# Four chained transformer layers on one core: attention scores by 64x64 quarters, two tiles at once, in layers 1 and 3; layer 2's loop written out; the end of layer 0 re-ordered

## The chip, the cores and the metric

The kernel runs on one core of a Trainium2 chip. The time is that of the device, in microseconds (us), and smaller is better. Three runs of the kernel before took 2104.95 to 2109.8 us, with a median of 2108.38 us.

## The reference

Sixty-four sequences of 64 tokens with 256 features pass through four layers, all in float32. Each layer normalises its rows, scales and shifts them by vectors made from a conditioning input, runs attention over the 64 tokens of each sequence, adds the result, and then does the same with an MLP of 1024 hidden features. What differs:

```python
# layer 0: one head of 256; RMS norm; GELU
scores = jnp.einsum('bnd,bmd->bnm', Q, K) * D ** (-0.5)
# layer 1: 16 heads of 16; RMS norm; rotary embedding of q and k; SwiGLU
q = _rope(q.reshape(B, T, n_head, hd)).transpose(0, 2, 1, 3)
k = _rope(k.reshape(B, T, n_head, hd)).transpose(0, 2, 1, 3)
attn = jnp.einsum('bhqd,bhkd->bhqk', q, k) * (1.0 / np.sqrt(hd))
# layer 2: 16 heads of 64 (qkv of 3 x 1024); layer norm; gated residual
attn = jnp.einsum('bqhd,bkhd->bhqk', q, k) * scale
# layer 3: 16 heads of 16; layer norm; padding mask; gated residual
mask = padding_mask[:, None, :] & padding_mask[:, :, None]
attn = jnp.where(mask[:, None, :, :], attn, -1000000000.0)
```

## The kernel before, in words

All rows (`xres`) stay in SBUF. They are cut into 8 blocks of 512 rows: 8 sequences, or 4 tiles of 128 rows. Eight phases follow each other, attention and MLP of the four layers (`PHASES`, line 52; phase 4 is layer 2's attention), and each phase goes over its 8 blocks. Weights of the next phase are loaded in shares and split by GpSimd into a rounded part and a rest (`share`, `split_next`, line 1307), and each projection is three matmuls, of rest by rounded, rounded by rest and rounded by rounded (`project`, line 630).

The order of the work is written by hand: `order_of` (line 78) returns for each kind of phase a list of stages. Each stage is marked as belonging to this block (`own`), the one before (`prev`) or the one after (`nxt`). `run_phases` (line 376) walks that list once per block, and every engine walks the same list and issues what its part of a stage is. So the list fixes the order on each engine, and semaphores (`n_at` gives the values) do the rest. The first and the last block of a phase are written out and the six between them are a loop (`Fori`, line 413); phase 0 is written out whole (line 406). At a phase's end the remaining `prev` stages are run inside the next phase, and `UP_AFTER` (line 145) says behind which of them the next MLP's first two `up` products go.

Attention of layers 1 and 3 has 8 steps a block, called slots here: slot k begins at `own("scores", k)`. Half c = k // 4 of the features (128 of 256, 8 heads) goes with tile j = k % 4 (two sequences). In a slot:

- PE makes the scores of tile k into its own PSUM bank, `scores[k % 2]`. The stationary operand is `qb`, q of one sequence with the heads of odd or even number zeroed (two copies, side by side). The moving operand is `kx`, which holds k of the sequence four times, each copy with only one group of 32 features (two heads) left and zeros elsewhere. So one product of 128 by 128 with 256 columns gives all eight heads, for one sequence (lines 727 to 730). In layer 3 a product of mask rows is added first (line 725).
- VectorE takes the maximum over keys (line 1217) and writes the scores less the maximum to `pb` (line 1220), then frees the bank.
- PE turns `pb` of the tile before (`probs_t`, line 741), ScalarE takes exp while it copies it to `pt` (line 994), PE multiplies with the values (`pv`, line 760; each head has a 17th column of ones), and VectorE divides after every second tile (lines 1239 and 1244).

Once a block: statistics (`stats`, line 1131; GpSimd makes rstd, line 1352), `norm` (line 1149 in layer 1, 1151 in layer 3), `turn` (PE transposes, line 675; VectorE scales, line 1159; GpSimd adds, line 1357), `split` (ScalarE `h_hi`, line 897; VectorE `h_lo`, line 1170), the projections q, k and v, `merge` of the heads (lines 782, 1001, 1251), `proj`, and `back` (PE line 826, VectorE line 1297, adds to `xres`). In layer 1 q and k are also rotated: ScalarE writes rows (line 903), SyncE swaps neighbouring partitions by DMA (line 545), VectorE multiplies by the cosine (line 1178), GpSimd by the sine and adds (lines 1362 and 1368). ScalarE's `q_out` makes the two copies of `qb` (line 965); `k_out` makes `kx` in four operations of 32 partitions (lines 950 and 959). Before the first use `kx` is zeroed by ScalarE (`zero_part`, line 852).

Layer 2 (heads of 64) already makes its scores with 64x64 quarters of the PE array (lines 712 to 719): 16 products a step, which the trace counts as 32 instructions, and its values likewise (line 774). In layer 0's last block GpSimd divides (line 1376), splits weights (`share`) and adds a bias to `xres` (`bias`, line 1386).

Of the kernel before, what the change touches and what calls it, by code (L numbers as in the profile page):

```python
# [77 lines left out]
def order_of(kind, layer):  # L78
# [37 lines left out]
    if layer == 3:  # L116
        return [own("mask", 1), own("scores", 0), prev("probs_t", 7), own("q", 1), own("q_out", 1), prev("pv", 6), own("share"), nxt("load"),
                own("scores", 1), own("probs_t", 0), own("v", 0), prev("pv", 7), own("v_out", 0), own("v", 1),
                own("v_out", 1), nxt("stats"),
                own("scores", 2), nxt("norm"), own("probs_t", 1), prev("merge"), own("k", 1), own("k_out", 1), own("pv", 0),  # L120
                own("scores", 3), own("probs_t", 2), prev("proj"), own("pv", 1), nxt("turn"),
                own("scores", 4), own("probs_t", 3), prev("back"), nxt("split"), own("pv", 2),
                own("scores", 5), nxt("mask", 0), own("probs_t", 4), own("pv", 3), nxt("k", 0), nxt("k_out", 0),
                own("scores", 6), own("probs_t", 5), own("pv", 4), nxt("q", 0), nxt("q_out", 0),
                own("scores", 7), own("pv", 5), own("probs_t", 6)]
# [17 lines left out]
TABLE_BANKS = (3, 5)  # L143

UP_AFTER = {0: [("probs_t", 0), ("pv", 0)], 1: [("merge", 0), ("proj", 0)],
# [19 lines left out]
def counts_of(kind, layer):  # L165
# [16 lines left out]
    if layer in (1, 3):  # L182
        c.update(o_full=n, o_inv=n // 2, o_free=n // 2, q=2 * 2, k=4 * 2, v=2 * 2, q32=2, w_full=3, w_free=1, att_hi=2, att=2)
    if layer == 1:
        c.update({f"{s}_{what}": 64 if what == "swapped" else 2 for s in "qk" for what in ("rows", "cos", "swapped", "sin")})
        c.update(k32=2)
# [11 lines left out]
def build(nc, x_in, cond_in, mask_k_in, mask_q_in, vec_in, modw_in, weights_in, out, phases=len(PHASES)):  # L198
# [13 lines left out]
    with ExitStack() as ctx:  # L212
# [18 lines left out]
        zeroed = ctx.enter_context(nc.semaphore("zeroed"))  # L231
        mask_made = ctx.enter_context(nc.semaphore("mask_made"))
# [40 lines left out]
        no_seq = place("no_seq", [P, 2], F32)  # L273
        mx = place("mx", [P, 2, SEQ], F32)
# [559 lines left out]
        def _(act):  # L834
# [36 lines left out]
            def stage_of(ph, s, k, b):  # L871
# [4 lines left out]
                if kind == "mlp" and layer in (0, 2) and s == "up" and k >= 3 and is_first(b):  # L876
                    if k == 3:
                        act.wait_ge(sem["x_done"], n_at("x_done", ph, 0, 1))
# [611 lines left out]
```

## Time and profile before

| | value |
|---|---|
| median of three runs | 2108.38 us |
| the profiled execution | 2108.39 us, span 2106.6 us |
| PE busy | 1998.5 us (95%), 15460 matmuls |
| VectorE, ScalarE, GpSimd busy | 1301.5, 1018.7, 439.5 us |
| layer 0 attention, MLP | about 137 and 208 us |
| layer 1 attention, MLP | about 288 and 267 us |
| layer 2 attention, MLP | about 534 and 206 us |
| layer 3 attention, MLP | about 269 and 198 us |
| mean granted clock of PE | 0.988 |

PE is the matmul side of TensorE, PEld its weight loads, DVE is VectorE, ACT ScalarE, POOL GpSimd, SP SyncE. Busy time of PE overlaps from one matmul to the next, so the distance between two starts says more than a duration. The clock is the share of 2.4 GHz that was granted; 0.5 is 1.2 GHz.

### The profile page before, as it was taken

The numbers are of one execution on the slowest core, as the hardware profiler recorded it, in microseconds if no ns is written. First come the engines' busy times: TensorE is split into PE (matmuls) and PEld (weight loads), VectorE is DVE, ScalarE is ACT, GpSimd is POOL, SyncE is SP. The second block draws the span as 40 slices with busy tenths as digits, with TensorE's granted clock in tenths as the row PEclk, the third lists the DMA queues.
The fourth block names the chain that finished last, engine by engine and source line by source line (L and its number), as shares of the span: only waits on it lengthen the run. The fifth ranks groups of instructions, "written<-read, shape, count | busy, mean of one in ns | idle before, by whom it ended". The sixth has DMA issues, their size and how long they took to land.

```text
span 2106.6 us, 44526 instructions
## 1 busy us (share of the span) xinstructions
PE 1998.5 (95%) x15460; PEld 1639.1 (78%) x15460; DVE 1301.5 (62%) x2506; ACT 1018.7 (48%) x1623; POOL 439.5 (21%) x409
## 2 busy tenths in 40 slices
PE   8989998989899999999999989998999999999998
PEld 7977887777777888877777777776888778787887
DVE  6665665777775656545544555555666777775664
ACT  4436555565643333335444444445446645554453
POOL 4441113445430101011111111111011321210000
PEclk9989999999999999999999999999999999999999
DMA  6000000111110000000000000000000000000000
GB/s 230 16 15 8 7 11 28 46 37 45 37 38 11 20 10 20 10 11 7 2 5 7 6 7 1 5 4 13 6 7 8 11 6 10 10 0 11 20 20 30
DMA packets 23959, 42.06 MB, mean 20 GB/s; under 512 B 2354, under 2 KB 13106, under 8 KB 23474
## 3 DMA queue, kind: packets, MB, share of 16 engines
q1 hardware_dynamic: 23858, 40.65, 5.8%
q8 instruction: 71, 1.16, 0.2%
q14 instruction: 30, 0.25, 0.0%
HBM read 28.06 MB, written 4.19 MB: 15 GB/s over the span
## 4 chain that ended last, share of the span: by engine, by line
PE 80%; DVE 8%; issue 7%; ACT 3%; POOL 1%; DVEq 0%; DMA 0%; ACTq 0%; POOLq 0%; SPq 0%
PE psum L633 21%; PE psum L635 19%; PE psum L634 19%; PE psum L728 4%; PE psum L741 3%; PE psum L675 3%; PE psum L760 2%; PE psum L826 2%; DVE xn L1149 2%; PE psum L774 2%; PE psum L717 1%; DVE pb L1220 1%; DVE mx L1217 1%; PE psum L564 1%; DVE h_lo L1170 1%
## 5 line engine op out<-in xcount | busy, mean ns | idle before, releaser
L633 PE MATMUL psum<-h_hi,w_lo 128*128 128x512 f32 x1056 | 433.9, 411 | 18.3 <-DVE h_lo L1170 7.6
L635 PE MATMUL psum<-h_hi,w_hi 128*128 128x512 f32 x1056 | 414.6, 393 | 0.0
L634 PE MATMUL psum<-h_lo,w_hi 128*128 128x512 f32 x1056 | 413.5, 392 | 0.0
L1272 DVE TENSOR_TENSOR hid_lo<-hid,hid_hi 128x512 fp32r<-128x512 f32 x256 | 193.0, 754 | 264.2 <-ACT hid_hi L1029 264.1
L1029 ACT ACTIVATE hid_hi<-hid 128x512 fp32r<-128x512 f32 x256 | 161.8, 632 | 219.4 <-PE psum L635 128.1
L1352 POOL TENSOR_TENSOR rstd<-ms,half_t 128x4 f32<-128x4 f32 x64 | 65.9, 1030 | 920.1 <-DVE ms L1144 474.6
L633 PEld LDWEIGHTS psum<-h_hi,w_lo 128*128 128x128 f32 x1056 | 199.2, 189 | 67.5 <-issue 16.5
L1217 DVE TENSOR_REDUCE mx<-psum 128x8 f32<-128x512 f32 x192 | 132.1, 688 | 168.0 <-PE psum L717 114.9
L635 PEld LDWEIGHTS psum<-h_hi,w_hi 128*128 128x128 f32 x1056 | 198.9, 188 | 44.0
L634 PEld LDWEIGHTS psum<-h_lo,w_hi 128*128 128x128 f32 x1056 | 199.8, 189 | 34.7
L1024 ACT ACTIVATE hid<-psum,vec 128x512 f32<-128x512 f32 x192 | 131.7, 686 | 163.9 <-PE psum L635 152.8
L633 PE MATMUL psum<-hid_hi,w_lo 128*128 128x512 f32 x512 | 200.0, 391 | 3.2 <-DVE hid_lo L1272 2.4
L635 PE MATMUL psum<-hid_hi,w_hi 128*128 128x512 f32 x512 | 199.6, 390 | 0.0
L634 PE MATMUL psum<-hid_lo,w_hi 128*128 128x512 f32 x512 | 199.2, 389 | 0.0
L1376 POOL TENSOR_TENSOR pb<-pb,ri 128x512 f32<-128x512 f32 x72 | 75.2, 1045 | 403.4 <-DVE ri L1232 403.4
L728 PE MATMUL psum<-kx,qb 128*128 128x256 f32 x512 | 142.2, 401 | 17.1 <-ACT qb L965 15.2
L994 ACT ACTIVATE pt<-psum 128x512 f32<-128x512 f32 x128 | 76.6, 598 | 131.5 <-PE psum L741 126.1
L741 PE MATMUL psum<-vec,pb 128*128 128x128 f32 x800 | 124.1, 279 | 14.3 <-ACTq L934 5.9
L1220 DVE TENSOR_TENSOR pb<-psum,mx 128x512 f32<-128x512 f32 x192 | 132.7, 691 | 6.6
L741 PEld LDWEIGHTS psum<-vec,pb 128*128 128x128 f32 x800 | 98.8, 143 | 41.6 <-issue 11.1
L728 PEld LDWEIGHTS psum<-kx,qb 128*128 128x128 f32 x512 | 95.4, 196 | 29.5 <-issue 18.2
L1170 DVE TENSOR_TENSOR h_lo<-hm,h_hi 128x512 fp32r<-128x512 f32 x120 | 87.0, 761 | 49.7 <-ACT h_hi L897 47.6
(143 smaller groups left out, 3675.0 us busy)
## 6 DMA issues: line engine op xcount, KB each, us to landing
swapped<-rows SPq DMA_DIRECT2D x64, 128.0 KB, 2.0
stage<-in_w_dram SPq DMA_DIRECT2D x24, 256.0 KB, 2.7
stage<-in_w_dram SPq DMA_DIRECT2D x8, 512.0 KB, 3.6
out_dram<-xres SPq DMA_DIRECT2D x8, 512.0 KB, 2.9
xres<-in_x_dram SPq DMA_DIRECT2D x1, 3072.0 KB, 15.3
modw_mod<-in_modw_dram SPq DMA_DIRECT2D x2, 1536.0 KB, 17.4
stage<-in_w_dram SPq DMA_DIRECT2D x8, 384.0 KB, 3.2
stage<-in_w_dram SPq DMA_DIRECT2D x8, 192.0 KB, 2.4
```

What stands on the lines that cost most here:

```text
L633: nc.tensor.matmul(dst, s_lo, m_hi, start=start and j == 0, stop=False)
L634: nc.tensor.matmul(dst, s_hi, m_lo, start=False, stop=False)
L635: ins = nc.tensor.matmul(dst, s_hi, m_hi, start=False, stop=stop and j == len(pairs) - 1)
L728: ins = nc.tensor.matmul(dst.rearrange("p (r g k) -> p r g k", g=2, k=S)[:, :, g, :], qb[:, c, 2 * j + g, :, :].rearrange("p h q -> p (h q)"),
L741: ins = nc.tensor.transpose(dst[:, t * P:(t + 1) * P], pb[:, slot, t * P:(t + 1) * P], ident)
L994: nc.scalar.activation(pt[:, slot, :], probs_tp, ACT.Exp, scale=SCORE_SCALE[layer]).then_inc(sem["probs_t"], 1)
L1024: nc.scalar.activation(hid32[:, slot, :], scores[slot], func, bias=col(f"u{layer}", k)).then_inc(sem["hid32"], 1)
L1029: nc.scalar.activation(hid_hi[:, slot, :], hid32[:, slot, :], ACT.Copy).then_inc(sem["hid_hi"], 1)
L1170: nc.vector.tensor_tensor(lo[:, m, :], hm[:, m, :], hi[:, m, :].bitcast(F32), ALU.subtract).then_inc(sem["h"], 1)
L1217: nc.vector.tensor_reduce(top, sc, AX.X, ALU.max).then_inc(sem["row_max"], 1)
L1220: nc.vector.tensor_tensor(dst, sc, top, ALU.subtract).then_inc(sem["shifted"], 1)
L1272: nc.vector.tensor_tensor(hid_lo[:, slot, :], hid32[:, slot, :], hid_hi[:, slot, :].bitcast(F32), ALU.subtract).then_inc(sem["hid"], 1)
```

## The change

It makes these edits:

1. Scores of layers 1 and 3: a new stage `pair` makes the scores of tiles k and k + 1 on PE in 64 instructions of 64x64. Tile u of the pair takes one half of both banks. `qb` now holds four copies of q, one for each head number modulo 4, and `kk` holds k once, with no copies and no zeros. VectorE begins either tile once the whole pair is done.
2. `q_out` has four ScalarE operations (times `is_head`, a table made at the start by two small VectorE operations) instead of two. `k_out` is gone in layer 1 (GpSimd's last addition writes `kk`) and one operation in layer 3.
3. The lists of layers 1 and 3 are rewritten: q and k of both halves are made for the next block in slots 4 to 7, statistics, norm and turn come later, `share` comes in slot 4, `back` at the end.
4. Phase 4 (layer 2's attention) is written out instead of looped.
5. End of layer 0: both first `up` products of the next phase go behind `divide`, and GpSimd's last `share` waits until the next phase's first h is done.
6. Only the value table is zeroed, at `up` 3; the eight operations on `kx` go.

```diff
     if layer == 1:
-        return [own("scores", 0), prev("probs_t", 7), prev("pv", 6), own("q_cos", 1), own("k_out", 1), nxt("stats"),
-                own("q_rot", 1),
-                own("scores", 1), own("probs_t", 0), own("v", 0), prev("pv", 7), own("v_out", 0), own("v", 1), own("v_out", 1),
-                nxt("norm"),
-                own("scores", 2), own("probs_t", 1), prev("merge"), nxt("turn"), own("q_out", 1), own("pv", 0),
-                own("scores", 3), own("probs_t", 2), nxt("split"), prev("proj"), own("pv", 1), own("share"), nxt("load"),
-                own("scores", 4), own("probs_t", 3), nxt("k", 0), nxt("k_swap", 0), prev("back"), own("pv", 2),
-                own("scores", 5), own("probs_t", 4), nxt("k_cos", 0), nxt("k_rot", 0), nxt("q", 0), nxt("q_swap", 0),
-                own("pv", 3),
-                own("scores", 6), own("probs_t", 5), nxt("q_cos", 0), nxt("k", 1), nxt("k_swap", 1), nxt("q_rot", 0),
-                nxt("k_out", 0), own("pv", 4),
-                own("scores", 7), own("probs_t", 6), nxt("k_cos", 1), nxt("q", 1), nxt("q_swap", 1), nxt("k_rot", 1),
-                nxt("q_out", 0), own("pv", 5)]
+        return [own("pair", 0), own("scores", 0), prev("probs_t", 7), prev("pv", 6), own("v", 0), prev("pv", 7),
+                own("scores", 1), own("probs_t", 0), own("v_out", 0), own("v", 1), own("v_out", 1), nxt("stats"), own("pair", 2),
+                own("scores", 2), own("probs_t", 1), nxt("norm"), prev("merge"), own("q_out", 1), own("pv", 0),
+                own("scores", 3), own("probs_t", 2), nxt("turn"), own("pv", 1), nxt("split"), prev("proj"), own("pair", 4),
+                own("scores", 4), own("probs_t", 3), nxt("q", 0), nxt("q_swap", 0), nxt("k", 0), nxt("k_swap", 0), own("pv", 2),
+                own("share"), nxt("load"),
+                own("scores", 5), own("probs_t", 4), nxt("q_cos", 0), nxt("k_cos", 0), nxt("q_rot", 0), nxt("k_rot", 0),
+                own("pv", 3), own("pair", 6),
+                own("scores", 6), own("probs_t", 5), nxt("q_out", 0), nxt("q", 1), nxt("q_swap", 1), nxt("k", 1),
+                nxt("k_swap", 1), own("pv", 4),
+                own("scores", 7), own("probs_t", 6), nxt("q_cos", 1), nxt("k_cos", 1), nxt("q_rot", 1), nxt("k_rot", 1),
+                own("pv", 5), prev("back")]
...
+UNROLLED = (0, 4)
...
-UP_AFTER = {0: [("probs_t", 0), ("pv", 0)], 1: [("merge", 0), ("proj", 0)],
+UP_AFTER = {0: [("divide", 0), ("divide", 0)], 1: [("merge", 0), ("proj", 0)],
...
-                if engine is None or ph == 0:
+                if engine is None or ph in UNROLLED:
...
+                elif s == "pair":
+                    for u in range(2):
+                        pe.wait_ge(sem[f"s_free{u}"], n_at(f"s_free{u}", ph, b, k // 2))
+                    pe.wait_ge(sem["q"], n_at("q", ph, b, 4 * (c + 1)))
+                    wait_alone(pe, sem["k"], n_at("k", ph, b, c + 1))
...
+                    for u in range(2):
+                        for x in range(2):
+                            for g in range(2):
+                                seq, o = 2 * (j + u) + g, (2 * x + g) * S
+                                for r in range(2):
+                                    rows = slice(r * S, (r + 1) * S)
+                                    for hd in range(2):
+                                        ins = nc.tensor.matmul(pair_scores(u)[hd * S:(hd + 1) * S, r, o:o + S],
+                                                               qb[rows, c, seq, 2 * x + hd, :],
+                                                               kk[rows, c, seq * S:(seq + 1) * S], start=layer == 1,
+                                                               stop=layer == 1 or u == x == g == 1)
+                        ins.then_inc(sem[f"s_full{u}"], 1)
...
-                        for hd, parity in enumerate(("even", "odd")):
-                            nc.scalar.activation(qb[:, k, :, hd, :], by_seq(q32[:, :]), ACT.Copy,
-                                                 scale=col(parity)).then_inc(sem["q"], 1)
+                        for head in range(4):
+                            nc.scalar.activation(qb[:, k, :, head, :], by_seq(q32[:, :]), ACT.Copy,
+                                                 scale=is_head[:, head:head + 1]).then_inc(sem["q"], 1)
...
+                    whole = slot if layer == 2 else 1
+                    dve.wait_ge(sem[f"s_full{whole}"], n_at(f"s_full{whole}", ph, b, k // 2 + 1))
...
+                    if ph == 0 and b == blocks - 1 and phases > 1:
+                        pool.wait_ge(sem["h"], n_at("h", 1, 0, 2))
                     split_next(ph, b)
```

Layer 3's new list has the same shape: `pair` 0, 2, 4 and 6 in the same places, q 0 and k 0 in slot 4, q 1 and k 1 in slot 6, `back` at the end, and its two `mask` stages at the head of the block and in slot 5. Its `pair` first adds the masks with four products of 256 columns.

## Rows read from the trace of the kernel before

**Rows 1.** Windows: length, busy us of PE, PEld, DVE, ACT, POOL; clock, DMA, GB/s.
```profile
426.80:530.60 103.80, 96.49 (x828) 79.07 (x828) 79.02 (x147) 62.51 (x102) 49.77 (x39) 0.97 0.12 42
1703.30:1803.30 100.00, 96.41 (x852) 79.18 (x852) 73.82 (x145) 53.06 (x85) 21.53 (x28) 1.00 0.03 8
```

**Rows 2.** Timeline of PE in layer 2: start us, us, line, operation, idle before.
```profile
1175.38 0.39 PE L634 MATMUL psum<-at_lo,w_hi 128*128 128x512 f32 x1
1175.61 0.39 PE L635 MATMUL psum<-at_hi,w_hi 128*128 128x512 f32 x1
1175.92 0.69 PE L717 MATMUL psum<-k_sb,q_sb 64*64 64x64 f32 x32
1176.77 0.69 PE L774 MATMUL psum<-pt,v_sb 64*64 64x64 f32 x32 [0.15 <-issue]
1177.40 0.50 PE L633 MATMUL psum<-h_hi,w_lo 128*128 128x512 f32 x1
```

**Rows 3.** Timeline of PE in layer 1, one tile's scores and what follows.
```profile
455.91 1.13 PE L728 MATMUL psum<-kx,qb 128*128 128x256 f32 x4
456.88 0.60 PE L741 MATMUL psum<-vec,pb 128*128 128x128 f32 x4
```

**Rows 4.** The same in layer 3.
```profile
1750.12 1.03 PE L728 MATMUL psum<-kx,qb 128*128 128x256 f32 x4
1750.99 0.60 PE L741 MATMUL psum<-vec,pb 128*128 128x128 f32 x4
```

**Rows 5.** Waits of PE in layer 1, 385 to 633 us: total, times, longest.
```profile
PE psum L728 <- ACT qb L965: 11.7, 6, 2.4
```

**Rows 6.** Timeline of VectorE in one block of layer 1.
```profile
465.38 1.40 DVE L1131 BATCH_NORM_STATS2 st<-xres 128x6 f32 x4 [0.28 <-DVE q L1178]
...
467.73 0.69 DVE L1217 TENSOR_REDUCE mx<-psum 128x8 f32<-128x512 f32 x1
...
469.39 0.26 DVE L1239 RECIPROCAL ri<-psum 128x16 f32<-128x16 f32 x1 [0.24 <-DVE pb L1220]
...
470.02 2.15 DVE L1149 TENSOR_SCALAR xn<-xres,rstd 128x256 f32 x4
...
473.74 1.41 DVE L1251 SCALAR_TENSOR_TENSOR at_lo<-psum,vec,at_hi 128x512 fp32r<-128x512 f32 x2 [0.24 <-ACT at_hi L1001]
475.60 1.29 DVE L1159 TENSOR_TENSOR hm<-psum,mod 128x512 f32<-128x512 f32 x2 [0.45 <-DVE at_lo L1251]
...
478.44 1.92 DVE L1170 TENSOR_TENSOR h_lo<-hm,h_hi 128x512 fp32r<-128x512 f32 x2 [0.23 <-DVE pb L1220]
```

**Rows 7.** Timeline of VectorE in layer 3: the norm.
```profile
1748.37 1.39 DVE L1151 TENSOR_SCALAR xn<-xres,mv,rstd 128x256 f32 x4 [0.15 <-DVE pb L1220]
```

**Rows 8.** PE in layer 1: k 0's first matmul, pv 7, and the stretch around 464 us.
```profile
445.90 0.49 PE L633 MATMUL psum<-h_hi,w_lo 128*128 128x512 f32 x1
...
467.92 0.66 PE L760 MATMUL psum<-vb,pt 128*64 128x34 f32 x16
...
461.00:468.00 7.00, 6.65 (x46) 5.54 (x48) 4.51 (x14) 3.81 (x7) 0.81 (x2) 0.76 0.10 37
```

**Rows 9.** Layer 2: three of its iterations (columns of rows 1), and a wait of PE.
```profile
1042.10:1105.00 62.90, 61.40 (x752) 49.30 (x752) 32.99 (x62) 29.73 (x50) 11.17 (x11) 1.00 0.02 4
1105.00:1174.00 69.00, 63.07 (x753) 50.54 (x753) 32.98 (x62) 29.61 (x50) 11.19 (x11) 0.98 0.02 6
...
1237.00:1306.60 69.60, 63.93 (x752) 51.13 (x753) 32.99 (x62) 29.60 (x50) 11.19 (x11) 0.95 0.02 6
...
1115.83 0.69 PE L717 MATMUL psum<-k_sb,q_sb 64*64 64x64 f32 x32 [2.42 <-issue]
```

**Rows 10.** End of layer 0: VectorE's norm, two waits of PE, and the clock.
```profile
130.78 5.43 DVE L1149 TENSOR_SCALAR xn<-xres,rstd 128x256 f32<-128x256 f32 x4 [0.32 <-POOL rstd L1352]
...
136.27 1.97 PE L675 MATMUL psum<-vec,xn 128*128 128x128 f32 x8 [3.80 <-DVE xn L1149]
...
149.63 1.11 PE L741 MATMUL psum<-vec,pb 128*128 128x128 f32 x4 [3.70 <-POOL pb L1376]
...
133.00:140.00 7.00, 3.73 (x13) 3.36 (x14) 5.63 (x6) 0.90 (x2) 3.06 (x2) 0.64 0.11 30
```

More of the change, by code:

```diff
@@ L116, in order_of @@
-    if layer == 3:
[L117 to L125, printed above, removed]
+        return [own("pair", 0), own("scores", 0), prev("probs_t", 7), prev("pv", 6), own("v", 0), prev("pv", 7),
[10 more added lines that the diff above has]
+                own("pv", 5), prev("back")]
@@ new lines, in order_of @@
+    if layer == 3:
+        return [own("mask", 1), own("pair", 0), own("scores", 0), prev("probs_t", 7), prev("pv", 6), own("v", 0), prev("pv", 7),
+                own("scores", 1), own("probs_t", 0), own("v_out", 0), own("v", 1), own("v_out", 1), nxt("stats"), own("pair", 2),
+                own("scores", 2), own("probs_t", 1), nxt("norm"), prev("merge"), own("pv", 0),
+                own("scores", 3), own("probs_t", 2), nxt("turn"), own("pv", 1), nxt("split"), prev("proj"), own("pair", 4),
+                own("scores", 4), own("probs_t", 3), nxt("q", 0), nxt("q_out", 0), nxt("k", 0), nxt("k_out", 0), own("pv", 2),
+                own("share"), nxt("load"),
+                own("scores", 5), nxt("mask", 0), own("probs_t", 4), own("pv", 3), own("pair", 6),
+                own("scores", 6), own("probs_t", 5), nxt("q", 1), nxt("q_out", 1), nxt("k", 1), nxt("k_out", 1), own("pv", 4),
+                own("scores", 7), own("probs_t", 6), own("pv", 5), prev("back")]
@@ L273, in build @@
         no_seq = place("no_seq", [P, 2], F32)
+        is_head = place("is_head", [P, 4], F32)
+        by_16 = place("by_16", [P, 8], F32)
         mx = place("mx", [P, 2, SEQ], F32)
@@ L312, in build @@
         mask_k8 = place("mask_k8", [P, blocks * BLK], U8, free3)
+        k0_sb = place("k0_sb", [P, DC, BLK], F32, free + 8192)
         q0_sb = place("q0_sb", [P, DC, BLK], F32, free)
@@ L695, in stage_of @@
                     ins.then_inc(full, 1)
-                elif s == "scores":
+                elif s == "pair":
[3 more added lines that the diff above has]
+                    wait_alone(pe, sem["k"], n_at("k", ph, b, c + 1))
+                    if layer == 3:
+                        pe.wait_ge(sem["mask_now"], n_at("mask_now", ph, b, c + 1))
+                        for u in range(2):
+                            for r in range(2):
+                                nc.tensor.matmul(pair_scores(u)[:, r, :].rearrange("p (x w) -> p x w", w=P),
+                                                 mask_q_now[:, c, j + u, :],
+                                                 mask_k_now[:, c, j + u, :].unsqueeze(1).to_broadcast([P, 2, P]),
+                                                 start=u == 0, stop=False)
+                    for u in range(2):
+                        for x in range(2):
+                            for g in range(2):
+                                seq, o = 2 * (j + u) + g, (2 * x + g) * S
+                                for r in range(2):
+                                    rows = slice(r * S, (r + 1) * S)
[5 more added lines that the diff above has]
+                        ins.then_inc(sem[f"s_full{u}"], 1)
+                elif s == "scores" and layer in (0, 2):
                     pe.wait_ge(sem[f"s_free{slot}"], n_at(f"s_free{slot}", ph, b, k // 2))
@@ L875, in stage_of @@
                     table_part(k)
[L876 to L879 removed]
+                if kind == "mlp" and layer in (0, 2) and (s, k) == ("up", 3) and is_first(b):
+                    act.wait_ge(sem["x_done"], n_at("x_done", ph, 0, 1))
+                    zero_values()
                 if PHASES[ph] == ("mlp", 2) and s == "up" and 2 <= k < 6 and isinstance(b, int) and b == blocks - 1:
@@ L884, in stage_of @@
                     mask_table(k - 2)
-                if is_first(b) and (s, k) == ("k_out", 0):
-                    act.wait_ge(zeroed, 5 if layer == 1 else 10)
                 if is_first(b) and (s, k) == ("v_out", 0):
                     act.wait_ge(prepared, 2 if layer == 1 else 4)
+                if is_first(b) and (s, k) == ("q_out", 0):
+                    act.wait_ge(heads_told, 2)
                 if s == "q" and ph == 0 and k == 0 and is_first(b):
@@ L1382, in stage_of @@
                     pool.wait_ge(sem["normed"], n_at("normed", ph, b, 1))
-                    if not isinstance(b, int) or b < blocks - 1:
+                    if b < blocks - 1:
                         pool.wait_ge(sem["h"], n_at("h", ph, b + 1, 2))
```

83 lines of the change are left out of this document (33 added, 50 removed).

## The prediction

> **What bounds the kernel now.** I read first the busy time of two stretches of three blocks each, one in layer 1's attention and one in layer 3's [rows 1]. PE is busy for 96.5 of 103.8 us and for 96.4 of 100.0 us. So a block takes 34.6 us in layer 1 and 33.3 us in layer 3, of which PE idles 2.4 and 1.2 us. PE is the bound in both, but VectorE stands right behind it: 79.0 and 73.8 us, 26.3 and 24.6 us a block. That second number is the one to keep in mind, because this change takes work from PE and none from VectorE. In layer 1 the granted clock is 0.97, which costs PE about 1.0 us a block.
>
> **Scores by quarters.** The new matmuls have the form of layer 2's scores and values. There [rows 2] a run of 32 instructions of 64x64 starts at 1176.77 and the next matmul at 1177.40: 0.63 us, so a pair of tiles (64 instructions) costs 1.26 us in two runs, and I take 1.2 us in one. Two tiles now cost 2 x 0.97 us in layer 1 [rows 3] and 2 x 0.87 us in layer 3 [rows 4]. A pair therefore saves 0.74 and 0.54 us, and four pairs a block save 3.0 and 2.2 us. The mask product keeps its columns (two of 512 become four of 256 a pair), so I cost it at nothing; at worst it adds two more weight loads a pair, hidden like the others. Entering the small form is not free: the matmul before a 64x64 run holds PE from 1175.61 to 1175.92 [rows 2], 0.31 us instead of the 0.23 us of its neighbours. That is 0.08 us a pair, which I charge: 2.7 and 1.9 us a block are left.
> The Trainium skill, TensorEngine Tiling (Array Packing), section Key Properties, says that a change of tiling mode drains TensorE, which speaks against this change. The trace agrees in kind, with the 0.08 us above, and the drain is too small to turn the sign.
> PE's floor is then 34.6 - 2.4 - 1.0 - 2.7 = 28.5 us a block in layer 1 and 33.3 - 1.2 - 1.9 = 30.2 us in layer 3.
>
> **q and k a slot sooner.** The largest idle time of layer 1 is the one before the block's first scores: PE waits for qb, 11.7 us in six times, 1.9 us each [rows 5]. With q and k of both halves projected before the block begins, and only q_out 1 left for slot 2, this wait goes. What is late next? The normed rows: statistics and norm move about a slot later (norm now stands behind scores 2), turn joins split in slot 3, yet q 0 moves up into slot 4, so PE's q 0 will wait for h_lo. I follow the ring of work that this closes, once round a block.
> On VectorE, beginning when PE has done the previous block's pv 7 [rows 6]: that pv 0.63 us (469.39 to 470.02) and 0.3 us to be released; scores 1, 1.6 us (467.73 to 469.39 with its wait); statistics 2.35 us (465.38 to 467.73); scores 2, 1.6 us; norm 1.4 us [rows 7] (2.1 us when GpSimd works beside it [rows 6], as it did in layer 1; in the new order GpSimd has nothing but rstd there); merge 1.4 + 0.2 us; scores 3, 1.6 us. Then turn, GpSimd's additions, ScalarE's h_hi and VectorE's h_lo, from 475.60 to 480.36, 4.7 us. Sum 15.8 us. All of it is in order on VectorE, and nothing of it can start before PE's pv 7, since scores 1 stands behind pv 7 in VectorE's order.
> On PE, from q 0 to that pv 7: the same stages take from 445.90 to 467.92 + 0.59 = 22.6 us now [rows 8], less the stall 1.9 and less (1 - 0.76) x 7.0 = 1.7 us of low clock in it, 19.0 us. It holds five tiles of scores (4.85 us) and one set of transposes (0.4 us) that become two pairs (2.4 us): 16.2 us. In layer 3 add two pairs' masks, each near 0.45 us since 512 columns take 0.23 us: 17.1 us.
> The ring is 32.0 us in layer 1 and 32.9 us in layer 3, above PE's floors of 28.5 and 30.2 us. So the ring, not PE, sets the new beat. In layer 1 I take it as it is: 2.6 us a block saved, 21 us over eight blocks. One thing could lengthen it: q_out has four ScalarE operations instead of two, ahead of q 1's and k 1's rows; k_out's four go, so ScalarE as a whole gets lighter, and I charge nothing but leave 1 us a block in the range. In layer 3 VectorE's part is shorter than the sum (its statistics have one step less, and fewer waits stand between), so I take 32.3 us, nearer to the ring than to the floor: 1.0 us a block, 8 us. The bounds are 0 and the floor in either layer: 0 to 49 us and 0 to 25 us.
> Other moves: `share` goes behind the turn, so GpSimd's split of weights comes after its additions; its load on SyncE now stands behind q 0's and k 0's swaps and waits for nothing new. The swaps keep their number, q first; no urgent transfer stands behind them. VectorE's k_cos waits for the last pair that reads its half of kk, done a slot earlier: nothing. `back` moves to the end of slot 7, still a slot and a half ahead of the merge that needs `wide`: nothing beyond its place in the ring. The first blocks' zeroing of kx (eight ScalarE operations) goes; no PE wait is shown for it, 0 us.
>
> **Layer 2 written out.** Its iterations take 62.9 us, but two of the six take 69.0 and 69.6 us [rows 9]. In those PE stands 2.42 us before the first scores with "issue" as its releaser and again before the next run, which is where the loop's branch is; nothing it needs is late. Written-out blocks before and after this loop show no such stop. I take both away: 6.1 + 6.7 = 12.8 us. Bounds 0 and, if each iteration loses some more register work, 18 us.
> The Trainium skill, Runtime: NRT & Kernel Launch, section Instruction fetch mechanics, says that a taken branch out of the fetched window forces a fetch before execution goes on. By that rule alone every iteration would stop; the trace shows two of six.
>
> **End of layer 0.** VectorE's norm for the next phase takes 5.43 us while GpSimd splits weights and adds the bias; PE idles 3.80 us for it [rows 10]. Holding `share` back until h is done leaves the norm alone at about 1.4 us [rows 7], 4.0 us less, nearly all of which PE waited for: 3.5 us saved. The other wait, 3.70 us for GpSimd's division, gets both first `up` products (2 x 1.4 us from six matmuls at 0.23 us) moved into it: 2.8 us. The clock there is 0.64 over 7.0 us, 2.5 us lost; I give back 1.7. The price is that `share` and `bias` of the last block come later; if they delay the division, half of this is lost. 8 us, bounds 2 and 12.
>
> **The sum.** 21 + 8 + 13 + 8 = 50 us off the profiled execution's 2108.4 us (span 2106.6 us), which is also the median of the runs: 2058 us.
>
> **Rivals.**
> (a) VectorE keeps up and the ring stays slack, because scores wait less than I think: PE's floors rule. 49 + 25 + 13 + 10 = 97 us, 2011 us. For it: PE's share of 95% and more now; against it: the wait for h_lo is already there with one slot more room.
> (b) Nothing is gained in layers 1 and 3: the ring is 2 us longer, through q_out's four operations and low clock after the new stall. Only 21 us are left: 2087 us. For it: a stop of 1.9 us brought the clock to 0.76 [rows 8].
> (c) The stops of layer 2 stay when it is written out, since all its instructions still come once: 2058 + 13 = 2071 us.
> (d) Slower. Scores used to have two banks that were freed one by one; now a pair needs both halves free, and VectorE may read neither tile until the pair is done. If PE waits at each of the 64 pairs, the 37 us of matmul time are spent at 0.6 us a pair and the whole 58 us (with layers 0 and 2) at 0.9 us. With 1.5 us a pair, 96 us: 2108 - 58 + 96 = 2146 us. Against it: between one pair's last reader and the next pair lie a projection or two of PE work, each 1.4 us or more.
> (e) No change worth naming, from gains and new waits that cancel.
>
> **How the numbers follow.** The forecast (2040 to 2070 us) has 0.52; (a) with what lies between it and the forecast 0.17; (b) 0.13; (c) 0.10; (d) 0.05; (e) 0.03. From 2022 to 2088 us I leave out most of (a)'s far half, (d), (e) and part of (b), 0.2 together; that width also covers the bounds of the single terms. A measurement of this kernel can tell 0.2% (4 us) from no change. Faster by more: 0.52 + 0.17 + 0.13 + 0.10 = 0.92; within: 0.03; slower: 0.05.
>
> **What would show it.** Right: runs of 64 small matmuls in about 1.2 us; no wait of PE for qb at the block's start; a new wait of PE for h_lo of 1 to 3 us before q 0, once a block; blocks of about 32 us in both layers; VectorE's share above 80% there; layer 2's iterations all near 62.9 us. Wrong: blocks under 30 us, or PE waiting for VectorE before pairs, or the two "issue" stops still there; runs of 64 that take 2 us or more would break the first step.

## The result, and the profile after

The changed kernel takes 2072.3 us (median of four runs, 2071.4 to 2072.9) where the kernel before took 2106.7 us in the same comparison (2096.9 to 2109.8): a ratio of 0.985 with a 95% interval of 0.983 to 0.988, some 34 us less. The profiled execution of after is 2072.0 us (span 2070.2), against 2108.4 us before. The forecast was 2058 us, a gain of 50 us. One of the six executions of the last experiment below took 2890.9 us at a granted clock of 0.61; it is left out of that run's time.

To see where the 36 us between the two profiled executions lie, take the start of the last residual write of each phase (VectorE's `xres`). A layer's first `q` and `k` are made within the phase ahead of it, so the MLP row ahead of an attention carries a little of that attention's work. Length of each phase in us, before and after:

| phase | before | after | difference |
|---|---|---|---|
| layer 0 attention | 159.8 | 148.8 | -11.0 |
| layer 0 mlp | 200.5 | 198.2 | -2.3 |
| layer 1 attention | 286.9 | 271.1 | -15.8 |
| layer 1 mlp | 282.1 | 282.0 | -0.1 |
| layer 2 attention | 520.9 | 502.0 | -18.9 |
| layer 2 mlp | 195.0 | 197.6 | +2.6 |
| layer 3 attention | 270.5 | 279.5 | +9.0 |
| layer 3 mlp | 186.3 | 186.4 | +0.1 |

Layers 0, 1 and 2 gained, each within some 6 us of its forecast. Layer 3 lost 11.6 us, with the MLP ahead of it. Here are two stretches of three blocks, one in layer 1 and one in layer 3, that answer to [rows 1], same columns.

```profile
442.90:542.40 99.50, 88.40 (x1517) 73.08 (x1508) 76.07 (x149) 53.76 (x91) 49.61 (x39) 0.98 0.13 44
1661.60:1765.00 103.40, 92.27 (x1551) 75.51 (x1548) 75.71 (x145) 47.50 (x78) 23.61 (x27) 1.00 0.03 8
```

PE is busy for 29.5 and 30.8 us a block, less than before (32.2 and 32.1) in both layers. The blocks last 33.2 and 34.5 us: PE idles 3.7 us in each. VectorE is at 76% and 73%. The bound is neither engine alone but the way the two wait for each other.

The timeline of PE around one pair in layer 1, against [rows 3]:

```profile
458.28 0.39 PE L638 MATMUL psum<-at_hi,w_hi 128*128 128x512 f32 x1
458.59 1.16 PE L719 MATMUL psum<-kk,qb 64*64 64x64 f32 x64
459.69 0.55 PE L758 MATMUL psum<-vec,pb 128*128 128x128 f32 x3
```

64 quarters take 1.10 us, and the matmul ahead of them 0.31 us. Next, PE's waits (total, times, longest), first in layer 1 from 385 to 609 us, against [rows 5]:

```profile
PE psum L636 <- DVE h_lo L1176: 10.8, 6, 1.8
PE psum L678 <- DVE xn L1155: 6.4, 7, 2.4
PE psum L758 <- DVE pb L1233: 5.7, 9, 0.8
PE psum L719 <- DVEq L1235: 1.4, 5, 0.3
```

The wait for `qb` is gone; a wait of 1.8 us for h_lo ahead of q 0 stands in its place. In layer 3, from 1661.6 to 1833.9 us (five blocks):

```profile
PE psum L636 <- DVE h_lo L1176: 5.6, 5, 1.1
PE psum L708 <- DVEq L1235: 5.1, 10, 0.8
PE psum L678 <- DVE xn L1157: 4.5, 5, 0.9
PE psum L758 <- ACT pt L996: 3.1, 5, 0.6
```

The kernel before had one wait of more than 0.3 us here in each block, 0.9 us for h_lo. Now there are five waits a block: one each for h_lo, the norm and the exp, and two at the pairs. The last line is ScalarE's timeline behind it:

```profile
1720.13 2.56 ACT L967 ACTIVATE qb<-q,is_head 128x512 f32<-128x512 f32 x4 [4.21 <-DVE q L1199]
1722.60 0.67 ACT L960 ACTIVATE kk<-psum,vec 128x512 f32<-128x512 f32 x1
1723.52 0.60 ACT L996 ACTIVATE pt<-psum 128x512 f32<-128x512 f32 x1 [0.25 <-ACT kk L960]
```

The exp that PE needs for its next transposes (L996 is the one into `pt`) stands behind five copies. The chain of waits in layer 3, from one block's pv 7 to the next stall (start, us, what), shows how the copies come into the ring:

```profile
1700.24 0.61 PE psum L777 x16
1700.88 0.27 DVE ri L1252
...
1706.92 0.18 DVE xn L1157
...
1714.67 0.64 ACT h_hi L909
...
1716.12 1.40 DVE y L1297 x2
...
1719.26 0.76 DVE q L1199
1720.13 0.14 ACT qb L967
...
1723.52 0.61 ACT pt L996
1724.17 0.66 PE psum L758 x4
```

From pv 7's end (1700.85) to PE's transposes (1724.17) it is 23.3 us. PE then works 11.1 us without a stop to the next block's pv 7. Together 34.4 us, the block.

Layer 2's iterations, against [rows 9]:

```profile
1039.10:1101.00 61.90, 60.57 (x753) 48.60 (x753) 32.89 (x62) 29.49 (x50) 11.15 (x11) 1.00 0.02 6
1101.00:1163.00 62.00, 60.65 (x753) 48.69 (x753) 32.89 (x62) 29.55 (x50) 11.15 (x11) 1.00 0.02 6
```

All are alike, and 1 us shorter than even the iterations without a stop before. The end of layer 0, against [rows 10]: VectorE's norm, then two waits of PE, then the clock.

```profile
131.53 1.92 DVE L1155 TENSOR_SCALAR xn<-xres,rstd 128x256 f32<-128x256 f32 x4 [0.32 <-POOL rstd L1365]
```
```profile
133.50 1.09 PE L678 MATMUL psum<-vec,xn 128*128 128x128 f32 x8 [0.28 <-DVE xn L1155]
...
144.54 0.66 PE L758 MATMUL psum<-vec,pb 128*128 128x128 f32 x4 [0.32 <-POOL pb L1389]
```
```profile
123.00:150.00 27.00, 24.20 (x188) 20.40 (x188) 18.93 (x37) 14.00 (x23) 12.73 (x10) 1.00 0.06 18
```

The norm fell from 5.43 to 1.92 us, the two waits from 7.5 to 0.6 us, and the clock stays full. Two smaller waits are new between them: 0.67 us for the weights of the share that was held back, and 1.53 us for the exp behind the second wait.

### The profile page after: what moved, and what is told of

It reads as the page before. It is cut to its first block, busy times and chain, and to the rows that moved or that the text cites. A ratio compares the mean times of both kernels' runs of the same rounds, so it can differ in the third digit from the quotient of the medians.

```text
span 2070.2 us, 50466 instructions
## 1 busy us (share of the span) xinstructions
PE 1954.2 (94%) x19108; PEld 1605.9 (78%) x19108; DVE 1292.4 (62%) x2508; ACT 971.5 (47%) x1567; POOL 442.8 (21%) x409
## 4 chain that ended last, share of the span: by engine, by line
PE 74%; DVE 13%; issue 6%; ACT 3%; POOL 2%; DVEq 1%; DMA 0%; POOLq 0%; SPq 0%; ACTq 0%
PE psum L636 20%; PE psum L638 19%; PE psum L637 19%; PE psum L758 3%; PE psum L843 2%; DVE pb L1233 2%; DVE mx L1230 2%; PE psum L777 2%; PE psum L678 2%; PE psum L745 2%; PE psum L791 1%; DVE xn L1155 1%; PE psum L719 1%; POOL hm L1370 1%; DVE hm L1165 1%
## 5 line engine op out<-in xcount | busy, mean ns | idle before, releaser
L636 PE MATMUL psum<-h_hi,w_lo 128*128 128x512 f32 x1056 | 433.1, 410 | 34.4 <-DVE h_lo L1176 22.4
L758 PE MATMUL psum<-vec,pb 128*128 128x128 f32 x800 | 128.4, 283 | 22.8 <-DVE pb L1233 9.6
L996 ACT ACTIVATE pt<-psum 128x512 f32<-128x512 f32 x128 | 76.4, 597 | 124.0 <-PE psum L758 120.0
L909 ACT ACTIVATE h_hi<-hm 128x512 fp32r<-128x512 f32 x120 | 71.5, 627 | 124.6 <-POOL hm L1370 77.6
L758 PEld LDWEIGHTS psum<-vec,pb 128*128 128x128 f32 x800 | 88.3, 141 | 44.7 <-issue 17.7
L636 PEld LDWEIGHTS psum<-hid_hi,w_lo 128*128 128x128 f32 x512 | 96.1, 188 | 20.6 <-DVE hid_lo L1285 0.5
```

Source lines behind the costliest of these rows:

```text
L636: nc.tensor.matmul(dst, s_lo, m_hi, start=start and j == 0, stop=False)
L758: ins = nc.tensor.transpose(dst[:, t * P:(t + 1) * P], pb[:, slot, t * P:(t + 1) * P], ident)
L996: nc.scalar.activation(pt[:, slot, :], probs_tp, ACT.Exp, scale=SCORE_SCALE[layer]).then_inc(sem["probs_t"], 1)
```

## The experiments

The kernel before, run beside each group, was at 2108.6, 2108.9, 2109.2 and 2109.2 us. Each experiment starts from the changed kernel (2072.3 us) unless it says otherwise. One caution for what follows: layer 1's attention took 269.9 to 273.9 us in the traces of the seven programs that share the changed kernel's order there, the changed kernel among them. A difference of less than 4 us between two traces shows nothing by itself; the length of the blocks says more.

**Layer 2: looped again.**

```
-UNROLLED = (0, 4)
+UNROLLED = (0,)
```

> The changed kernel with layer 2's attention looped again, nothing else. If the written-out blocks are worth what the two profiles say, layer 2 gets back its two long iterations (69 and 69.6 us) and about 1 us in each of the other four: 18 to 20 us more than the changed kernel, near 2091 us, ratio to the kernel before near 0.993. If only the two stops count, 13 us more. If the writing out was worth nothing and layer 2 gained from something else, about 2072 us.

2114.5 us, ratio 1.002 (1.001 to 1.004): 42 us more than with the blocks written out, twice what was expected. Two iterations, and PE's two stops in one of them:

```profile
1039.00:1109.00 70.00, 63.59 (x752) 50.84 (x751) 32.62 (x63) 29.34 (x50) 11.16 (x11) 0.95 0.03 9
1109.00:1179.00 70.00, 63.91 (x757) 51.08 (x756) 33.70 (x64) 30.43 (x52) 11.16 (x11) 0.98 0.02 6
```
```profile
1096.19 0.30 PE L745 MATMUL psum<-k_sb,q_sb 64*64 64x64 f32 x2 [2.48 <-issue]
1098.84 1.02 PE L745 MATMUL psum<-k_sb,q_sb 64*64 64x64 f32 x28 [2.35 <-issue]
```

The five distances between looped blocks are now 69.1 to 70.5 us, with such a pair of stops in each; in the kernel before, two of the same five had it. The stops thus belong to the loop, not to the work. What decides that they come at two returns in one program and at all five in another was not found.

**Layer 2 written out, alone, in the kernel before.**

```
-                if engine is None or ph == 0:
+                if engine is None or ph in (0, 4):
```

> The kernel before with layer 2's blocks written out and nothing else. Theory: the two iterations at 68.8 and 69.6 us fall to some 63, and the others lose the branch's stop of up to 1 us: 13 to 19 us, run 2089 to 2095 us, iterations all within 0.5 us. Rival: the stops move to the loops of layers 1 and 3, whose code stands elsewhere now, and the run stays above 2100 us.

2089.3 us, ratio 0.990 (0.989 to 0.992): 19.7 us.

```profile
1005.90:1067.90 62.00, 60.67 (x754) 48.67 (x753) 32.86 (x62) 29.51 (x50) 11.16 (x11) 1.00 0.02 6
1067.90:1129.90 62.00, 60.67 (x753) 48.64 (x753) 32.88 (x63) 29.50 (x50) 11.16 (x11) 1.00 0.02 6
```

Over half of the whole change's gain is this line. The stops did not move to another loop: the other phases of this run are within 0.7 us of those before.

**End of layer 0 as it was.**

```
-UP_AFTER = {0: [("divide", 0), ("divide", 0)], ...
+UP_AFTER = {0: [("probs_t", 0), ("pv", 0)], ...
...
-                    if ph == 0 and b == blocks - 1 and phases > 1:
-                        pool.wait_ge(sem["h"], n_at("h", 1, 0, 2))
```

> The changed kernel with the end of layer 0 as it was before: the first two parts of the mlp's up come behind probs_t 0 and pv 0, and the share of weights does not wait for the split. Theory: the re-ordered end is worth the 11 to 11.5 us by which the two traces differ there, run 2083 to 2084 us; the waits of 3.8 and 3.7 us at the end of layer 0 come back. Rival: part of it came from elsewhere, run 2076 to 2080 us.

2082.5 us (2079.4 to 2085.8): 10.2 us more, and both old waits are back. The run undoes both edits at once; what each is worth by itself is not shown.

```profile
PE psum L678 <- DVE xn L1155: 3.8, 1, 3.8
PE psum L758 <- POOL pb L1389: 3.7, 1, 3.7
```

**Layer 3: the order of before, with pairs.**

```
-own("scores", 4), own("probs_t", 3), nxt("q", 0), nxt("q_out", 0), nxt("k", 0), nxt("k_out", 0), own("pv", 2),
+own("scores", 3), own("probs_t", 2), prev("proj"), own("pv", 1), nxt("turn"), own("pair", 4),
+own("scores", 4), own("probs_t", 3), prev("back"), nxt("split"), own("pv", 2),
...
```

> The changed kernel with layer 3's list put back to the order of the kernel before, its scores still made in pairs (pair 0, 2, 4, 6 ahead of scores 0, 2, 4, 6), q_out with four operations. If the order is what made layer 3's blocks go from 33.4 to 34.5 us (the ring over VectorE and back), the block comes to 31 to 32.5 us, less than the 33.4 us of the kernel before by the 1.9 us of matmul time or a little less, and the whole to 2072 - 7 x 2.5 = about 2055 us. If the pairs themselves or their barrier are the cause, the block stays at 34 us or more and the time at 2070 us or above.

2089.5 us (0.991, 0.989 to 0.993), 34 us above the expectation. Two of its blocks, then four together:

```profile
1684.70:1719.90 35.20, 30.56 (x519) 24.95 (x517) 24.60 (x48) 15.71 (x26) 7.14 (x10) 1.00 0.02 7
1719.90:1759.50 39.60, 34.91 (x519) 27.91 (x517) 24.61 (x48) 15.72 (x26) 7.19 (x11) 0.87 0.02 7
1684.70:1832.50 147.80, 129.19 (x2066) 104.80 (x2064) 98.44 (x192) 62.84 (x104) 28.65 (x37) 0.94 0.02 7
```

A block lasts 37.0 us on average, 2.5 more than in the new order. So it is not the new order that costs layer 3 its time: this is the other branch of the expectation, the pairs, their barrier or the copies that they need. PE waits 1.35 us for h_lo and 2.8 us for `qb` at the block's first pair in each block; where the clock was halved behind these waits the block lasts up to 4.4 us more (39.6 against 35.2). In this order the old scores did better (33.4 us a block) than the pairs.

**Turn one stage sooner, in layer 1, then in layer 3.** The next block's turn moved behind `merge`, its split behind scores 3.

```
-own("scores", 2), own("probs_t", 1), nxt("norm"), prev("merge"), ...
-own("scores", 3), own("probs_t", 2), nxt("turn"), own("pv", 1), nxt("split"), ...
+own("scores", 2), own("probs_t", 1), nxt("norm"), prev("merge"), nxt("turn"), ...
+own("scores", 3), own("probs_t", 2), nxt("split"), own("pv", 1), ...
```

> The changed kernel with one stage moved in layer 1: turn goes ahead of scores 3 (and split directly behind it), so that GpSimd's additions run beside scores 3. Ring theory: VectorE's part of the ring gets shorter by scores 3, 1.4 us, PE's wait for h_lo of 1.8 us falls to under 0.6 us, the low clock after it goes, and a block takes 31.0 to 32.0 us instead of 33.2: about 10 us less in all, 2062 us. If PE's own work or the pair barrier sets the beat, the wait only moves to another place and the time stays within 3 us of 2072.

> The same move in layer 3 alone. Here the profile's chain goes from VectorE's h_lo on through y, scores 4 and q 0 to ScalarE's four q_out operations, not to PE, so the order on VectorE matters only by the 0.6 us and 0.6 us that it idles around split. Ring theory: 0.8 to 1.2 us a block, 6 to 9 us in all, near 2065 us. If ScalarE's queue behind q_out sets the beat by itself, under 3 us.

Both missed: 2083.6 us in layer 1 (2072 before the move), 2074.5 us in layer 3. In layer 1 the waits for scores 2, norm and h_lo became one of 2.65 us for the norm, once a block, and two blocks in sequence read:

```profile
413.20:448.00 34.80, 31.41 (x500) 26.14 (x500) 27.00 (x51) 18.22 (x31) 16.05 (x13) 0.90 0.12 41
448.00:481.20 33.20, 29.94 (x500) 25.13 (x500) 26.24 (x51) 17.97 (x31) 16.07 (x13) 0.95 0.13 44
```

The work is the same; at a mean clock of 0.90 instead of 0.95 the block takes 1.6 us more. In layer 3 it was alike: 33.6 us at full clock, 0.85 less than in the changed kernel and so what the theory gave, but 36.0 at 0.91. The waits for norm and h_lo had become one of 2.2 us there too.

**Layer 3: the exp ahead of the copies.** q_out 0 and k_out 0 moved behind probs_t 4.

```
-nxt("q", 0), nxt("q_out", 0), nxt("k", 0), nxt("k_out", 0), own("pv", 2),
+nxt("q", 0), nxt("k", 0), own("pv", 2),
...
-own("probs_t", 4), own("pv", 3), own("pair", 6),
+own("probs_t", 4), nxt("q_out", 0), nxt("k_out", 0), own("pv", 3), own("pair", 6),
```

> Layer 3 of the changed kernel: the four copies of q_out 0 and the one of k_out 0 stand behind the exp of tile 4 on ScalarE (q_out 0 and k_out 0 two stages later). Theory: PE's wait of 0.61 us before probs_t 5 comes from these five instructions (about 3.2 us) ahead of that exp, and it goes: layer 3's block 34.45 to some 33.9 us, the run 2067 to 2070 us. Rival: PE meets the next wait in the row (pair 6, or the pair of the next block), and the run stays within 2 us of 2072.

2067.6 us (0.980, 0.978 to 0.982), blocks of 33.8 us instead of 34.45, as the first theory had it. PE's wait for the exp is gone. The run is 4.7 us faster; between the two traces layer 3's attention is 6.2 us shorter, and layer 1's, which the edit leaves alone, 2.8 us longer.

**Statistics a stage sooner, in both layers.**

```
-prev("probs_t", 7), prev("pv", 6), own("v", 0), prev("pv", 7), ... own("v_out", 1), nxt("stats"), own("pair", 2),
+prev("probs_t", 7), prev("pv", 6), nxt("stats"), own("v", 0), prev("pv", 7), ... own("v_out", 1), own("pair", 2),
```

> Layers 1 and 3 of the changed kernel, with one stage of their lists moved: the next block's squares and sums (VectorE, two instructions, about 2.3 us) stand ahead of v 0 and the last pv of the block before, where VectorE waits 1.85 us for pv 7, instead of between v_out 1 and the pair of tiles 2. Theory (ring): a block lasts as long as the ring from pv 7 over VectorE's scores, norm, turn, h_lo, y, q 0, ScalarE's q_out and the exp of tile 4, to PE; the two instructions leave its VectorE part (15.5 to 15.7 us), so a block of layer 1 takes some 31.4 us instead of 33.3, one of layer 3 some 32.3 instead of 34.5, and the run some 2045 to 2055 us. Rival (PE's own work with its half-clock stretches, or ScalarE's queue, sets the beat): the wait only moves, blocks within 0.3 us, run within 4 us of 2072.

2089.5 us (2081.2 to 2093.3): 17 us slower, and the theory fell. VectorE in layer 3 of this run:

```profile
1724.68 0.68 DVE L1230 TENSOR_REDUCE mx<-psum 128x8 f32<-128x512 f32 x1
1725.39 0.69 DVE L1233 TENSOR_TENSOR pb<-psum,mx 128x512 f32<-128x512 f32 x1
1728.13 0.69 DVE L1230 TENSOR_REDUCE mx<-psum 128x8 f32<-128x512 f32 x1 [2.05 <-PE psum L719]
```

The statistics did leave the stretch between pv 7 and the norm. But what sets the norm's time is scores 1 on VectorE, then pair 2 on PE (it needs both halves of the scores free), then scores 2 on VectorE, and only then the norm. Taking work out of VectorE beside PE's pair only makes VectorE idle there (2.05 us). In layer 3 the block stayed at 34.6 us. In layer 1 VectorE had less room ahead of scores 1: it came later, PE waited up to 2.7 us at pair 2, and the clock was 0.94 instead of 0.98 over three blocks.

**Layer 3: use that gap.** Statistics as above, the norm ahead of scores 2, turn and split a stage sooner, and the exp ahead of the copies.

```
+own("mask", 1), own("pair", 0), own("scores", 0), prev("probs_t", 7), prev("pv", 6), nxt("stats"), own("v", 0), prev("pv", 7),
+... own("pair", 2),
+nxt("norm"), own("scores", 2), own("probs_t", 1), prev("merge"), nxt("turn"), own("pv", 0),
+own("scores", 3), own("probs_t", 2), nxt("split"), own("pv", 1), prev("proj"), own("pair", 4),
...
```

> Layer 3 of the changed kernel: squares and sums of the next block ahead of v 0, its norm ahead of scores 2 (VectorE idles 2.05 us there while PE works on the pair of tiles 2), its turn one stage sooner (behind merge), the split behind probs_t 2, q_out 0 and k_out 0 behind the exp of tile 4. Theory (the path of a block goes from VectorE's scores 1 over PE's pair 2 back to VectorE's scores 2 and only then to the norm, so only a norm ahead of scores 2 shortens it): the norm ends some 3 us sooner, PE's waits of 0.90 us at the turn, 1.13 us ahead of q 0 and 0.61 us ahead of probs_t 5 go, those at the pairs (0.8 and 0.7 us) stay, a block of layer 3 takes 31.8 to 32.4 us instead of 34.45, and the run 2054 to 2060 us. Rival (the time of a block is set by VectorE's and ScalarE's work whatever the order): block 33.6 to 33.8 us as with q_out moved alone, run 2066 to 2069 us.

2059.6 us (0.977, 0.976 to 0.979): 12.8 us below the changed kernel, the fastest of all. Three blocks, VectorE's norm in the gap, and PE's waits over five blocks:

```profile
1658.20:1756.60 98.40, 91.05 (x1550) 75.46 (x1548) 75.16 (x144) 47.17 (x78) 23.81 (x27) 1.00 0.03 8
```
```profile
1698.50 1.38 DVE L1157 TENSOR_SCALAR xn<-xres,mv,rstd 128x256 f32 x4 [0.15 <-DVE pb L1233]
1700.39 0.69 DVE L1230 TENSOR_REDUCE mx<-psum 128x8 f32<-128x512 f32 x1 [0.52 <-PE psum L719]
```
```profile
PE psum L708 <- DVEq L1235: 11.1, 15, 1.1
PE psum L636 <- DVEq L1268: 1.2, 5, 0.2
```

A block is 32.8 us, 0.4 above the upper end of what I expected: the waits for norm, h_lo and exp are gone, those at the pairs add up to 2.2 us a block where I had counted 1.5. Layer 3's attention and the MLP ahead of it now take 463.8 us, against 465.5 in the kernel before and 477.1 in the changed one: the loss is gone, and hardly anything is gained on the kernel before. Four stages moved at once here; their single shares, and what this order would do for the old scores, were not tried.

**Layer 1: the turn's product ahead of scores 3.**

```
-own("scores", 3), own("probs_t", 2), nxt("turn"), own("pv", 1), nxt("split"), ...
+own("probs_t", 2), nxt("turn"), own("scores", 3), own("pv", 1), nxt("split"), ...
```

> Layer 1 of the changed kernel: VectorE does the turn's product with the modulation ahead of scores 3 instead of behind them; nothing else moves. Theory: h_lo ends some 1.5 us sooner, PE's wait of 1.8 us ahead of q 0 shrinks to at most 0.4 us, the stretch at half clock behind it goes (1.4 us), and up to 0.4 us comes up at the pair of tiles 4, which waits for scores 3: a block of layer 1 takes 30.5 to 32.0 us instead of 33.3, the run 2060 to 2066 us. Rival (as when the whole turn was moved a stage up): the wait only moves, to the pair of tiles 4, and the clock still falls, the run 2070 us or more.

> Both edits together (layer 3 with norm, turn and q_out 0 re-ordered, layer 1 with the turn's product ahead of scores 3). Theory: the two gains add, since the two layers are different stretches of the time: 2072 less the sum of what each gives alone, some 2045 to 2054 us. Rival: at most one of the two gains holds, 2060 us or more.

2074.3 and 2062.7 us: nothing gained in layer 1, by itself or on top of the edit in layer 3. The wait for h_lo stayed, not at the pair as the rival said. VectorE's h_lo, and GpSimd at that time:

```profile
458.60 2.90 DVE L1176 TENSOR_TENSOR h_lo<-hm,h_hi 128x512 fp32r<-128x512 f32 x2
```
```profile
457.90 0.82 POOL L1333 CAST w_hi<-stage 128x768 f32 x1
458.90 2.05 POOL L1335 TENSOR_TENSOR w_lo<-stage,w_hi 128x768 f32 x1 [0.17 <-POOL w_hi L1333]
```

h_lo began 0.7 us sooner in its block, and its second half took 2.30 us; it takes 0.68 with GpSimd idle. It ends at 461.50, some 0.55 us after GpSimd's subtraction (460.95). The Trainium skill, SBUF — State Buffer, section SBUF: two separate sides, says that VectorE's instructions with two SBUF inputs and GpSimd's that read SBUF exclude each other for a whole instruction. The trace agrees: h_lo's second half ends nearly as if it had begun only when GpSimd was done.

**GpSimd's share moved away from h_lo.** Both edits, and `share` behind the rotation of q and k:

```
-own("pv", 2), own("share"), nxt("load"),
-own("scores", 5), own("probs_t", 4), nxt("q_cos", 0), nxt("k_cos", 0), nxt("q_rot", 0), nxt("k_rot", 0),
+own("pv", 2),
+own("scores", 5), own("probs_t", 4), nxt("q_cos", 0), nxt("k_cos", 0), nxt("q_rot", 0), nxt("k_rot", 0),
+own("share"), nxt("load"),
```

> Both edits together, and in layer 1 GpSimd's share of splitting the next weights moved behind its rotation of q and k (L1375, L1381), so that it no longer runs beside VectorE's h_lo. Theory: with the turn's product ahead of scores 3, the second h_lo took 2.30 us, until GpSimd's split of 768 columns (2.05 us) ended, where it takes 0.68 alone; with GpSimd idle there h_lo ends some 1.5 us sooner, PE's wait of 1.8 us ahead of q 0 falls under 0.5 us and the half clock behind it goes: a block of layer 1 of 30.5 to 31.8 us instead of 33.3, the run 2044 to 2052 us. Rival 1 (the length of h_lo has nothing to do with GpSimd): h_lo stays over 2 us for the second half, run 2058 to 2064. Rival 2 (the share is late for its buffer or delays the next rotation): h_lo falls but waits come up at the pair of tiles 0 or before scores, run over 2053.

2064.1 us (0.979, 0.977 to 0.980), against 2062.7 without this move. The mechanism held and the gain didn't come. VectorE's h_lo, and two blocks of layer 1:

```profile
457.50 1.28 DVE L1176 TENSOR_TENSOR h_lo<-hm,h_hi 128x512 fp32r<-128x512 f32 x2
```
```profile
440.70:472.80 32.10, 28.80 (x500) 23.91 (x500) 25.06 (x50) 17.99 (x31) 15.76 (x13) 1.00 0.14 45
507.50:541.80 34.30, 31.42 (x500) 26.18 (x500) 24.95 (x50) 18.04 (x31) 15.77 (x13) 0.90 0.12 42
```

Both halves take 0.68 us and the wait before q 0 is gone. In its place PE waits 1.2 us for scores 2 and 1.2 us for the norm, one right behind the other: GpSimd's rotation of q 1 and k 1, which waits for the swapped rows, ends at 450.0 us, 1.1 us after the statistics (448.9), so rstd starts that much later than it could. Where the clock stayed full the block is 32.1 us, shorter than any of the changed kernel; where it fell to 0.90, with nearly the same waits, 34.3. Three of the five blocks were at 0.90.

## Why the prediction was right in part

**Pairs.** I took 1.2 us for 64 quarters and 0.08 us for entering the form; measured 1.10 and 0.08. The four mask products take 0.53 us from the first one's start to the quarters' start, against 2 x 0.23 before. The saving on PE is there: 2.7 us of busy time a block in layer 1, 1.4 in layer 3 (forecast 2.7 and 1.9).

**Layer 1: the ring, right in kind.** The wait for qb went, a wait of 1.8 us for h_lo came once a block (forecast 1 to 3). The ring's VectorE part was put at 15.8 us; from pv 7's end at 446.47 to q 0 at 462.13 it measures 15.7. Its PE part was put at 16.2 us. The trace has two lengths for it, 18.0 us where the clock was halved behind the new wait and 16.9 where it stayed full, though the wait was 1.8 us in both. At the low clock the twelve matmuls of q 0 and k 0 take 4.35 us (462.13 to 466.48) instead of 2.8; at full clock PE meets another short wait instead, 0.35 to 0.42 us for VectorE's division. So the half clock, which I had put at nothing behind the new wait, is the larger part of the missing term, and not all of it: blocks of 33.7 and 32.6 us, where I had 32.0. A block went from 34.8 to 33.2 us on average, 1.6 instead of 2.6 saved. The first and last blocks, which I had not costed apart, gave 7.7 us more and the phase ahead 2.3, so that 21 us became 18.

**Layer 3: the step that failed.** I forecast 8 us less and it is 11.6 more (with the MLP ahead, into which its first steps reach). In the terms of the sum: VectorE's part was put at 15.8 us and takes 15.5 (1700.85 to q 0 at 1716.33). PE's part was put at 17.1 us and takes 18.9 (to the next pv 7's end at 1735.28), since I had counted it as work without a wait, and two waits stand in it, 0.74 us at pair 6 and 0.61 us for the exp. I had then taken 0.6 us off the sum of 32.9; it is 34.45. "The ring" that I built from layer 1's stages left VectorE at h_lo and came to PE's q 0. In layer 3 it goes on: h_lo, y, scores 4, q 0's product on VectorE, four copies of q_out and one of k_out on ScalarE, and the exp behind them. I had written of q_out's four operations in layer 1 "I charge nothing", and in layer 3 I did not name them; ahead of that exp stand 3.2 us of copies. The run with the exp first gives 0.65 us a block back and the one that also puts the norm into VectorE's gap 1.65. Rival (b) named this cause, without the loss. The second failure is in how a ring is summed. Adding up one engine's busy times between two points held for layer 1's length, but it does not tell what a move is worth: at pair 2 the path changes to PE and back, and statistics beside it cost nothing. The run with the earlier statistics fell on this.

**Barrier of the pairs, rival (d).** PE waiting for VectorE before pairs was one of my signs of being wrong, and it is there: 0.28 us (layer 1) and 1.0 us (layer 3) a block, far from 1.5 us at each pair. It did not decide the sign, but it is what remains as the largest wait once the others are gone (2.2 us a block).

**Layer 2.** 12.8 us forecast for the two stops, 18.9 by the traces and 19.7 by the run that does this alone; the missing 6 us are about 1 us in each of the six iterations, those with stops included. I had named it as "some more register work" and left it out of the forecast, and even my upper bound of 18 us lay a little under what came. The run with the loop put back shows a larger thing: in the changed program the loop would cost 42 us. Behind my forecast stood the trace of two stops in six. The Trainium skill, Runtime: NRT & Kernel Launch, section Instruction fetch mechanics, expects a stop where a branch's target is out of the fetched window. The run with the loop agrees with it, with a stop at every return; the kernel before, with two, shows that the same loop can also go through without one.

**Layer 0.** 8 us forecast, 11.0 by the traces, 10.2 by the run that undoes it. Both waits went almost wholly and the clock came back fully. The price was small: GpSimd's bias held the division up by some 0.4 us (143.05 to 143.44), and PE waited 0.67 us for the share that came later.

**VectorE's share** was to be above 80% in both layers and is 76% and 73%: the blocks stayed longer than forecast. Summed up: layer 1 -18, layer 2 -19, layer 0 -11, layer 3 +12, against -21, -13, -8 and -8 forecast. The stated range of 2022 to 2088 us would have held without the surplus in layers 0 and 2 (2081 us then): it was wide enough for the error in layer 3. The band to which I gave the largest chance, 2040 to 2070 us, was missed by 2 us. That it was so near is luck: two errors one way hid a part of one the other way.

Open: why layer 3's first and last blocks lost 3.5 us, why the loop stops when it does, and how far the four copies rather than the pair's barrier cost layer 3, since pairs without four copies were not tried. In layer 1 no run undid the pairs or the order alone, so how its 18 us divide between them is read from the trace and not shown by a run.

## What to carry to other kernels

When work is taken off the engine that bounds a kernel, follow one block's chain through every queue it passes and write down where it changes engine. Then ask of each stage you would move whether the chain waits beside it anyway. Put the producer that another engine waits for ahead of copies in an in-order queue, and fill the gap in which an engine waits for its partner with the next stage that is ready. Before crediting a re-ordering, check a loop's iterations one by one: here the loop was worth 19 us, and new scores and orders in two layers 6 us together.

## What the runs showed of the hardware

- The same block with the same instructions took 32.1 us at full clock and 34.3 us at a mean of 0.90. Waits of 1.2 to 2.7 us were followed by stretches at 1.2 instead of 2.4 GHz, in some blocks and not in others: in the changed kernel the same wait of 1.8 us stands in five blocks of layer 1, and the clock fell behind three of them.
- A loop's stop on PE: 2.48 and 2.35 us, at all five returns of the loop in one program and at two of them in another.
- VectorE's subtraction of two SBUF operands took 0.68 us alone and 2.30 us beside one GpSimd subtraction of 768 columns. In the changed kernel VectorE's two operations on scores, which read PSUM, took 0.68 and 0.69 us beside the same subtraction (461.62 to 463.70).
- 64 instructions of 64x64 on the quarters of the PE array took 1.10 us in a row, and the full-size matmul ahead of them 0.31 instead of 0.23 us.
